# AdaLN block with channel attention and a mixture of experts: normalisations moved from VectorE to ScalarE, and the tail of attention computed through one extra weight product

## What is computed

```python
mod = (silu(c) @ wmod).reshape(16, 6, 1, 128)          # sa, ca, ga, sb, cb, gb per batch
h   = layernorm(x) * (1 + ca) + sa
q, k, v = h @ Wq.T + bq, h @ Wk.T + bk, h @ Wv.T + bv  # 16 heads of 8 channels
q = softmax over the 8 channels of a head;  k = softmax over the 512 tokens
state = k^T v per head (8 x 8);  o = q state           # 128 channels again
o = (o - mean(o)) * rsqrt(var(o) + eps) * ln_g + ln_b
x = x + ga * (o @ Wo.T + bo)
h = layernorm(x) * (1 + cb) + sb
x = x + gb * moe(h)                                    # 8 experts 128->128 (gelu)->128, top 2 of 8
```

## Time and profile before

| | us |
|---|---|
| median of 3 runs | 433.97 (433.52 to 435.66) |
| the profiled execution, its own time | 437.05 |
| its span | 435.1 |
| PE, DVE busy | 386.1 (89%), 347.0 (80%) |
| ACT, POOL busy | 250.5 (58%), 214.7 (49%) |
| distance of two steps in the loop | 48.6 |

### The profile page before, as it was taken

How to read it: one execution, slowest core, us unless ns; L and a number is a source line. 1 busy time by engine, 2 the same in 40 slices (tenths; PEclk the granted TensorE clock), 3 DMA queues, 4 the chain that set the end, 5 groups by cost and what they waited for, 6 DMA issues and landing times.

```text
span 435.1 us, 8603 instructions
## 1 busy us (share of the span) xinstructions
PE 386.1 (89%) x2660; PEld 343.7 (79%) x2660; DVE 347.0 (80%) x1176; ACT 250.5 (58%) x390; POOL 214.7 (49%) x222
## 2 busy tenths in 40 slices
PE   4545858998999999998989999998989999999995
PEld 3444656988988888888979888888889888989895
DVE  4577889888898989888888988898888889885631
ACT  2433447565657476575667485675667475675541
POOL 3421525364545465464645465464645564664442
PEclk9968589899999999999999999999999999999999
DMA  6720023060505124160605033140605042234160
GB/s 198 264 94 28 2 89 133 2 219 26 218 26 177 66 68 150 35 207 24 218 24 205 37 103 116 49 194 25 217 24 194 26 141 80 95 127 164 58 217 26
DMA packets 17787, 47.51 MB, mean 109 GB/s; under 512 B 2067, under 2 KB 4966, under 8 KB 17510
## 3 DMA queue, kind: packets, MB, share of 16 engines
q1 hardware_dynamic: 17568, 46.84, 30.5%
q10 hardware_dynamic: 198, 0.41, 0.2%
HBM read 42.76 MB, written 4.48 MB: 109 GB/s over the span
## 4 chain that ended last, share of the span: by engine, by line
PE 34%; DVE 30%; issue 15%; POOL 5%; ACT 5%; DVEq 1%; POOLq 0%; ACTq 0%
PE pY L626 14%; DVE xn L758 4%; PE pH L614 3%; DVE top L857 3%; PE pH L615 3%; PE pH L616 3%; DVE v L883 3%; ACT u L452 3%; DVE xn L846 2%; POOL rstd L347 2%; DVE qs L782 2%; DVE qmax L778 2%; DVE kmax L764 2%; POOL v L335 2%; DVE qs L773 2%
## 5 line engine op out<-in xcount | busy, mean ns | idle before, releaser
L626 PEld LDWEIGHTS pY<-wout,v 128*128 128x128 f32 x1024 | 127.4, 191 | 9.1 <-DVE v L883 3.6
L626 PE MATMUL pY<-wout,v 128*128 128x128 f32 x1024 | 132.7, 276 | 1.3 <-DVE v L883 0.5
L452 ACT ACTIVATE u<-pH,cols 128x512 f32<-128x512 f32 x128 | 86.6, 686 | 63.6 <-PE pH L616 63.0
L883 DVE TENSOR_TENSOR v<-u,gate_bc 128x512 f32<-128x512 f32 x80 | 59.4, 745 | 24.6 <-ACT u L452 10.7
L335 POOL TENSOR_TENSOR v<-u,gate_bc 128x512 f32<-128x512 f32 x48 | 62.4, 1301 | 31.2 <-ACT u L452 13.0
L614 PE MATMUL pH<-h_hi,win_hi 128*128 128x512 f32 x128 | 59.5, 465 | 9.2 <-ACT u L452 9.2
L615 PE MATMUL pH<-h_hi,win_lo 128*128 128x512 f32 x128 | 51.0, 398 | 0.0
L616 PE MATMUL pH<-h_lo,win_hi 128*128 128x512 f32 x128 | 50.6, 395 | 0.0
L846 DVE TENSOR_SCALAR xn<-x_all,mv,rstd 128x128 f32 (+1 forms) x64 | 35.7, 619 | 14.0 <-POOL rstd L347 14.0
L325 POOL TENSOR_TENSOR rstd_o<-ve_o,neg_half 128x4 f32<-128x4 f32 x16 | 16.3, 1017 | 52.6 <-DVE ve_o L816 52.6
L347 POOL TENSOR_TENSOR rstd<-ve,neg_half 128x4 f32<-128x4 f32 x16 | 22.3, 1396 | 38.8 <-DVE ve L840 38.7
(11 more groups left out here) (142 smaller groups left out, 868.4 us busy)
## 6 DMA issues: line engine op xcount, KB each, us to landing
gate_bc<-route_scratch SPq DMA_DIRECT2D x64, 512.0 KB, 5.3
x_all<-in_L_attn_x SPq DMA_DIRECT2D x16, 256.0 KB, 6.4
out<-x_all SPq DMA_DIRECT2D x16, 256.0 KB, 2.0
gates<-gate_scratch SPq DMA_DIRECT2D x1, 2048.0 KB, 7.0
gb_bc<-gb_scratch SPq DMA_DIRECT2D x1, 1024.0 KB, 4.3
win<-in_L_ffn_w_in SPq DMA_DIRECT2D x1, 512.0 KB
wout<-in_L_ffn_w_out SPq DMA_DIRECT2D x1, 512.0 KB
wmod_sb<-in_L_wmod ACTq DMA_DIRECT2D x1, 384.0 KB, 3.6
```

Of the source, the lines that this page charges most:

```text
L452: act.activation(u[:, e % U, :], pH[:, e % 2, :], ACT.Gelu_apprx_tanh, bias=cols[:, e:e + 1]).then_inc(s["gelu_done"], 1)
L626: i = mm(pY[:, t * P:(t + 1) * P], v[:, e % U, t * P:(t + 1) * P], wout[:, e, :], start=False, stop=(e == NE - 1), skip_group_check=True)
L883: dve.tensor_tensor(v[:, e % U, :], u[:, e % U, :], gate_bc[:, par, e, :], ALU.mult).then_inc(s["v_done"], 1)
```

## The change

Every line below is from the diff; a line of "..." stands where it is cut.

- The two applications of a normalisation leave DVE (`tensor_scalar`, subtract mean, multiply) and become four ACT activations each, Identity with a per-partition scale (rstd) and bias (minus mean times rstd). DVE computes that bias in one small operation (`ln1_offset`, `ln2_offset`). On ACT, `ln1_apply(b+4)` stands between gelu 4 and gelu 5, `ln2_apply(b+2)` at the end of the step, so ahead of gelu 0 of the next step.
- `state` gives the transposed state; DVE only masks it (`s2T`). A new PE product, `state_weights`, multiplies it by two matrices side by side, [centred, gained and gated output weight | centring matrix]; ACT scales the 256 columns by 1/sum and brings them to SBUF (`sw_evac`). `attend` then takes turned q as weights, one tile of tokens at a time, against each half: the centred output goes to pQT (first), the projection to pC, both token-major.
- ACT squares the centred output, DVE sums it (`tensor_reduce`); `ssq`, `project`, `outT_evac` and the steps L804 to L812 go.
- The value bias is added where v is brought to SBUF, by DVE (`v_bias`) in place of ACT (`v_evac`).
- `qv` of the next batch now waits for the square (its bank is used for the centred output).
- In the setup, the output weight gets its centring by one more product, for which PE and DVE wait.

```diff
 (pool, rstd_L and rstd_B)
+                w(pool, "xn1_ready", T * n)
...
+                w(pool, "xn2_ready", T * n)
 (pool, gated_const)
-                pool.tensor_tensor(wog[:, :], wo_gain[:, :], gates[:, n, 0, :], ALU.mult).then_inc(s["wog_ready"], 1)
+                w(pool, "sw_done", n)
+                pool.tensor_tensor(sw_rhs[:, 0, :], wo_gain[:, :], gates[:, n, 0, :], ALU.mult).then_inc(s["wog_ready"], 1)
 (act)
+            def ln1_apply(n):
+                act.wait_ge(s["nmr1_ready"], n + 1)
+                w(act, "hT_done", n)
+                for t in range(T):
+                    act.activation(xn1[:, t, :], x_all[:, n, t, :], ACT.Identity, bias=nmr1[:, t:t + 1], scale=rstd1[:, t:t + 1]).then_inc(s["xn1_ready"], 1)
...
-            def v_evac(n):
...
-                act.activation(sq[:, :], pC[:, :], ACT.Square).then_inc(s["sq_ready"], 1)
-                act.activation(outT[:, :], pC[:, :], ACT.Copy).then_inc(s["outT_ready"], 1)
+            def sw_evac(n):
+                act.wait_ge(s["sw_done"], n + 1)
+                act.wait_ge(s["kinv_ready"], n + 1)
+                w(act, "out_done", 2 * n)
+                act.activation(sw[:, :, :].rearrange("p a c -> p (a c)"), pSW, ACT.Copy, scale=kinv[:, 0:1]).then_inc(s["sw_ready"], 1)
+
+            def out_square(n):
+                act.wait_ge(s["out_done"], 2 * n + 1)
+                w(act, "ssum_done", n)
+                act.activation(sq[:, :, :].rearrange("p t c -> p (t c)"), pQT, ACT.Square).then_inc(s["sq_ready"], 1)
 (act, step)
                 if B:
                     h2_evac(b + 1, nxt)
+                if A2:
+                    sw_evac(b + 2)
                 if M:
                     gelu(b, 2)
                     gelu(b, 3)
                 if A2:
-                    outT_evac(b + 2)
+                    out_square(b + 2)
...
                 if M:
                     gelu(b, 4)
+                if L:
+                    ln1_apply(b + 4)
+                if M:
                     gelu(b, 5)
-                if A1:
-                    v_evac(b + 3)
...
                     qT_evac(b + 3)
+                if A2:
+                    ln2_apply(b + 2)
 (pe)
             def qv(n):
-                w(pe, "qT_ready", n)
+                w(pe, "sq_ready", n)
...
-                    i = mm(pS, ek[:, t, :], v_sb[:, t, :], start=(t == 0), stop=(t == T - 1))
+                    i = mm(pS, v_sb[:, t, :], ek[:, t, :], start=(t == 0), stop=(t == T - 1))
+            def state_weights(n):
+                pe.wait_ge(s["s2T_ready"], n + 1)
+                pe.wait_ge(s["wog_ready"], n + 1)
+                mm(pSW, s2T[:, :], sw_rhs[:, :, :].rearrange("p a c -> p (a c)"), start=True, stop=True).then_inc(s["sw_done"], 1)
             def attend(n):
-                pe.wait_ge(s["s_ready"], n + 1)
+                pe.wait_ge(s["sw_ready"], n + 1)
                 pe.wait_ge(s["qT_ready"], n + 1)
-                mm(pC[:, :], s3[:, :], qT[:, :], start=True, stop=True).then_inc(s["out_done"], 1)
+                for half, o in ((1, pQT), (0, pC)):
+                    for t in range(T):
+                        i = mm(o[:, t * P:(t + 1) * P], qT[:, t * P:(t + 1) * P], sw[:, half, :], start=True, stop=True)
+                    i.then_inc(s["out_done"], 1)
 (pe, step)
                     combine(b - 1, nxt, 5)
+                if A2:
+                    state_weights(b + 2)
                 if B:
                     h2T(b + 1)
...
-                if A2:
-                    ssq(b + 2)
...
-                if A2:
-                    project(b + 2)
 (dve)
-            def ln1_apply(n):
+            def ln1_offset(n):
                 dve.wait_ge(s["rstd1_ready"], n + 1)
+                w(dve, "xn1_ready", T * n)
+                dve.scalar_tensor_tensor(out=nmr1[:, :], in0=mv1[:, :, 0], scalar=-1.0, in1=rstd1[:, :],
+                                         op0=ALU.mult, op1=ALU.mult).then_inc(s["nmr1_ready"], 1)
...
+            def v_bias(n):
+                dve.wait_ge(s["qv_done"], n + 1)
+                w(dve, "state_done", n)
+                dve.tensor_tensor(v_sb[:, :, :], pQV[:, :, 1, :], bv_bc[:, :].unsqueeze(1).to_broadcast([P, T, P]),
+                                  ALU.add).then_inc(s["v_ready"], 1)
...
+                dve.tensor_tensor(s2T[:, :], pS, blockmask[:, :], ALU.mult).then_inc(s["s2T_ready"], 1)
...
-                dve.wait_ge(s["ssq_done"], n + 1)
-                dve.tensor_scalar(ve_o[:, :], pSSQ, 1.0 / C, LN_EPS, ALU.mult, ALU.add).then_inc(s["veo_done"], 1)
+                dve.wait_ge(s["sq_ready"], n + 1)
+                dve.tensor_reduce(ssum[:, :], sq[:, :, :], AX.X, ALU.add).then_inc(s["ssum_done"], 1)
+                dve.wait_ge(s["ssum_done"], n + 1)
+                dve.tensor_scalar(ve_o[:, :], ssum[:, :], 1.0 / C, LN_EPS, ALU.mult, ALU.add).then_inc(s["veo_done"], 1)
...
                     q_shift(b + 3)
+                    v_bias(b + 3)
                 if A2:
                     out_var(b + 2)
 (dve, setup; pe has the product between)
+                dve.tensor_scalar(gain[:, :], woT[:, :], cols[:, NE + 1:NE + 2], None, ALU.mult).then_inc(s["gain_ready"], 1)
+                dve.tensor_scalar(cen[:, :], ident[:, :], 1.0 / C, None, ALU.subtract).then_inc(s["cen_ready"], 1)
+                dve.tensor_scalar(sw_rhs[:, 1, :], ident[:, :], 1.0 / C, None, ALU.subtract)
+                dve.wait_ge(s["mm_gain"], 1)
+                dve.tensor_copy(wo_gain[:, :], pA[:, 0:P]).then_inc(s["wo_gain_ready"], 1)
```

More of the change, by code:

```diff
@@ L67, in adaln_block @@
         woT = sb("woT", [P, P])
+        gain = sb("gain", [P, P])
         wo_gain = sb("wo_gain", [P, P])
@@ L412, in h2_evac, with ln2_apply @@
                 act.activation(h2_hi[:, par, :], pB[:, :], ACT.Identity, bias=modB[:, par, 1:2], scale=modB[:, par, 0:1]).then_inc(s["h2hi_ready"], 1)
+            def ln1_apply(n):
[3 more added lines that the diff above has]
+                    act.activation(xn1[:, t, :], x_all[:, n, t, :], ACT.Identity, bias=nmr1[:, t:t + 1], scale=rstd1[:, t:t + 1]).then_inc(s["xn1_ready"], 1)
+            def ln2_apply(n):
+                act.wait_ge(s["nmr2_ready"], n + 1)
+                w(act, "h2T_done", n)
+                for t in range(T):
+                    act.activation(xn2[:, t, :], x_all[:, n, t, :], ACT.Identity, bias=nmr2[:, t:t + 1], scale=rstd2[:, t:t + 1]).then_inc(s["xn2_ready"], 1)
             def exp_k(n):
@@ L513, in _ @@
             pe.wait_ge(s["attn_w_ready"], 2)
+            pe.wait_ge(s["gain_ready"], 1)
+            pe.wait_ge(s["cen_ready"], 1)
+            mm(pA[:, 0:P], cen[:, :], gain[:, :], start=True, stop=True).then_inc(s["mm_gain"], 1)
+            pe.wait_ge(s["wo_gain_ready"], 1)
             def router_here():
@@ L603, in gate_turn @@
                 pe.wait_ge(s["gate2_ready"], n + 1)
-                w(pe, "veo_done", n + 2 if not isinstance(n, int) else min(n + 2, NB))
                 for t in range(T):
@@ L840, in ln2_var, with ln2_offset @@
                 dve.tensor_scalar(ve2[:, :], mv2[:, :, 1], LN_EPS, None, ALU.add).then_inc(s["ve2_done"], 1)
-            def ln2_apply(n):
+            def ln2_offset(n):
                 dve.wait_ge(s["rstd2_ready"], n + 1)
-                w(dve, "h2T_done", n)
-                for t in range(T):
-                    dve.tensor_scalar(xn2[:, t, :], x_all[:, n, t, :], mv2[:, t, 0:1], rstd2[:, t:t + 1],
-                                      ALU.subtract, ALU.mult).then_inc(s["xn2_ready"], 1)
+                w(dve, "xn2_ready", T * n)
+                dve.scalar_tensor_tensor(out=nmr2[:, :], in0=mv2[:, :, 0], scalar=-1.0, in1=rstd2[:, :],
+                                         op0=ALU.mult, op1=ALU.mult).then_inc(s["nmr2_ready"], 1)
             def route(n):
@@ L909, in step @@
                 if L:
-                    ln1_apply(b + 4)
+                    ln1_offset(b + 4)
                 if M:
@@ L943, in step @@
                 if A2:
-                    ln2_apply(b + 2)
+                    ln2_offset(b + 2)
             def moe_gates_here():
```

67 lines of the change are left out of this document (17 added, 50 removed).

## The result

The changed kernel takes 441.74 us in the median of four runs (440.5 to 444.11), against 433.88 for the kernel before in the same comparison (433.52 to 435.66, four runs): a ratio of 1.0165, interval 1.0117 to 1.0213. It is slower by 1.65%, and outside my range of 423 to 439. The profiled executions took 441.16 (after) and 437.05 (before); the latter stood 3.1 above its median, so between the two traces only 3.8 us of span can be explained, and the medians say 7.9.

A forecast was written before the change was run, and what follows sets the result against it. PE, 95% busy, nearly bounds the loop, alongside a chain of waits through DVE and ACT. Loop 12 x -0.52, end -0.4, start +2.4: -4.2 on 437.05 gives 432.8, or 430.3 against the median; own range 428 to 433, full range 423 to 439.

The forecast's parts named there:

- Stretch 2: PE from the start of `hidden` 6 to the end of the next `kT`: 12.77 us plus 0.43 for `state_weights`, 13.20.
- PE without a gap: Claim that PE works through the 12.77 us from `hidden` 6 to the end of the next `kT` without waiting.
- worth nothing by itself: Claim that taking `ln2_apply` and the masking and scaling chain off DVE gains nothing there, as PE was the chain.
- Stretch 1: From the end of `kT` to `hidden` 6, through DVE and ACT: 11.52 us less 0.95 for the first normalisation, 10.57.
- A: Rival: DVE reaches kshift before POOL starts `h2_low`, saving 1.0 of kshift; loop about 23.1, time 422 to 424; chance 0.15.
- So the PE saving stays unused: Between `kT` and `hidden` 6, PE's work falls to about 9.5 us, but the chain stays with DVE and ACT.
- Activations: The four ACT activations of one normalisation: 0.46 us each at 0.35 distance, 1.5 us together.
- fit by 0.3 to 0.4: Gelu 0 ends 19.7 us after `kT`, `h_lo` at 22.4, before `hidden` 2 (20.0) and the next `kT` (22.8) need them.
- rival B: The loop's gain is eaten by late logits or gelu 0: period 24.0 to 24.2, time 434; chance 0.20.
- Rival C: ACT becomes the loop, `ln2_apply` delaying gelu 0 and `kT`: period near 24.5, time 440, slower; chance 0.20.
- Start: Steps before the full loop: +1.75 in step -2, +3.1 in step -1, -2.5 in step 0, together +2.4 us.
- End: After the loop, PE's work, one more step with A2: -0.4 us.

The follow-up runs named there:

- e1: The changed kernel run again with nothing altered: 444.02 us, ratio 1.0206 to the kernel before.
- e2: The changed kernel with POOL making the gained weight of the next batch before the second rstd: 436.84 us, ratio 1.0034 to the kernel before.
- e3: The kernel before with only the two normalisations moved to ACT, old tail of attention kept: 426.5 us, ratio 0.9797.
- e5: The kernel before with only the first normalisation moved to ACT: 427.48 us, ratio 0.9815.
- e10: The kernel of e3 with kbmax and kshift made one operation with a single SBUF input: 422.26 us, ratio 0.971 to the kernel before.
- e11: The kernel of e8 with kbmax and kshift made one operation with a single SBUF input: 424.06 us, ratio 0.9734 to the kernel before.
- e6: The kernel before with only the second normalisation moved to ACT: 436.64 us, ratio 1.0038.
- e8: The kernel of e2 with DVE's value bias moved behind the router's gates: 435.32 us, ratio 0.9988 to the kernel before.

## Why the prediction was wrong

By its steps, in the profiled executions:

- *Stretch 2, "12.77 + 0.43 = 13.20": this is the step that failed.* It counted the 0.43 us of `state_weights` and no wait in front of it. Of its two inputs I looked at neither: I did not ask when POOL's product L321 is ready once its reader moves to the head of the stretch, though POOL's order was before me. Before, that product ended at 211.78 and `state_weights` would have stood at 212.86; by the forecast's own shifts (the second rstd 0.1 later after `kT`, PE 0.95 earlier) that leaves 0.05 to spare, so even my own numbers would have shown a place with nothing in reserve. Measured are waits of 0.76 and 0.25 in turn, on average 0.50 (0.67 counted by starts), and a stretch 2 of 13.86 and 13.35, on average 13.60. In the medians the wait is worth 7.2 us beside e1, and 5.7 by the ratios to before (1.0165 and 1.0034, of 434), of the 11.4 by which 430.3 was missed; in the eleven steps of the traces it is 2.9 of the 6.4 that they miss (11 x 0.58).
- *That 13.20 is near the 13.26 of e2 is luck.* Two errors cancel in it. The base of 12.77 was not "PE without a gap": it held 0.31 of waiting for DVE, which goes with the second normalisation (12.46 in e3), where the prediction has it "worth nothing by itself". And behind `state_weights`, which takes 0.43 as forecast when it need not wait, stand 0.18 for gelu 0 and 0.18 for `h_lo`: 12.46 + 0.43 + 0.36 = 13.25.
- *Stretch 1, "11.52 - 0.95 = 10.57": right in kind, short by 0.2.* The exponential of q comes 203.02 - 194.94 = 8.08 after `kT`, for 7.89. I took kshift as unchanged, and in the step shown it was; but kbmax ahead of it, 0.20 before, became 0.36, and in the other kind of step 1.10 with a kshift of 0.16. A freed DVE reaches POOL's last operations one operation sooner, and then waits for their ends. e5 shows the same with nothing else changed. Taking the pair out is worth 0.55 a step in e10 and 1.0 in e11, with the order of `weigh` 2 and `h2_low` in it. I had put A, the rival in which the lock falls away, down to luck with the order; kshift's hold has to be removed by hand, and what is then left is a matter of the order, in e10 of 0.02 to 0.05 us.
- *"So the PE saving stays unused": right.* `hidden` 6 waits 1.48 for gelu 4, for the "about 1" of the forecast (0.78 before).
- *Activations, "1.5" for four: 1.63 to 1.65.* Single ones took 477 to 503 ns, and `sw_evac` 0.48. The Trainium skill's estimate (ScalarE: Activation LUTs, What ACT_TABLE_LOAD costs), which the prediction gave beside my own, was the better one; the trace agrees with it to a hundredth. The activations of `ln2_apply` and what follows, in the timelines of ACT, POOL and PE of the changed kernel:

```profile
213.04 1.65 ACT L428 ACTIVATE xn<-x_all,nmr,rstd 128x128 f32 x4 [1.49 <-DVE nmr L862]
214.60 0.67 ACT L470 ACTIVATE u<-pH,cols 128x512 f32<-128x512 f32 x1
...
216.67 1.28 POOL L346 TENSOR_TENSOR h_lo<-h,h_hi 128x512 fp32r<-128x512 f32 x1 [1.54 <-ACT h_hi L409]
...
218.62 0.48 PE L558 MATMUL pA<-h_hi,wk_hi 128*128 128x512 f32 x1
```

- *Gelu 0 and `h_lo` "fit by 0.3 to 0.4": wrong by about 0.5, and hidden by the wait.* Gelu 0 ends at 215.27, 20.3 after `kT` (forecast 19.7), and `h_lo` at 217.95, 23.0 after it (forecast 22.4). In the changed kernel `kT` still starts at 218.62 without a wait, but only because PE itself was held up at `state_weights`. In e2, where it was not, both come too late, by 0.18 each. That is the mechanism of rival B, on top of the one that no rival had. Rival C, in which ACT becomes the loop and whose time of 440 comes near the measured one, did not happen. C had the sign right and the mechanism wrong: moving the normalisations to ACT is the half that pays (e3). The Trainium skill's rule against it (ScalarE: Activation LUTs, Rules for kernel authors) does not hold for this kernel: with both on ACT e3 ran at 0.9797 of before, while ACT went from 58% busy to 69%. For the second move alone it is not contradicted: e6 took 436.64, no gain.
- *Start "+2.4": 2.3, with some luck.* Its parts were +1.75, +3.1 and -2.5, at the starts of `k_max` +0.85, +3.7 and -2.3. In e1, the same kernel, the sum was +4.1 (99.54 - 95.44), so the hit to a tenth is not more than one execution. In step -1 the row that I wrote down in advance is what the timeline of ACT shows, one behind the other:

```profile
67.39 1.65 ACT L428 ACTIVATE xn<-x_all,nmr,rstd 128x128 f32<-128x128 f32 x4 [0.91 <-DVE nmr L862]
69.06 1.28 ACT L470 ACT_TABLE_LOAD   x1
```

- *End "-0.4": +1.5, a miss of 1.9.* At the end of the profile `state_weights` waits for POOL too (the longest of the waits row, 1.4). In e8, with the weight made early and the value bias moved, what follows the last `k_max` takes 71.7, the 71.8 of before.
- *The sum against one execution.* The forecast of 432.8 was for an execution that began at 437.05 and was measured as 441.16. The further 3.1 us that I took off, to come to the median, did not apply to the changed kernel: its profiled execution stood 0.6 below its own median.

By the traces, then, the forecast for the execution missed by 8.4: 6.2 of gain in the loop that did not come, 1.9 at the end, 0.3 outside the span, and nothing at the start.

In short: half of the change gains 8.5 us, the other costs 15 to 18, some two fifths of it one wait of PE for a product of POOL that used to be needed late. Without that wait the eleven steps still take 8.3 us more than in e3 (264.89 for 256.62), and stretch 2 accounts for it: 13.26 for 12.46, `state_weights` itself and two short waits. In the medians the new tail costs 8.8 in e8 over e3, and 1.8 in e11 over e10, because without the pair of small operations its shorter work on PE in stretch 1 comes into use.

## What to carry to other kernels

When a change gives an operand a new reader, or moves its reader forward, follow each input of the new reader back through its producer's queue, even where that producer is at 49% and its operation is unchanged: slack belongs to a pair of writer and reader, not to an engine. And when a wait is removed, look for the next ones behind it: here half of its length came back. A change of two halves is worth timing in halves; here the sum hid a gain of 2% under a loss of about 4%. And where a small operation is many times longer than its size explains and ends with another engine's, time gained ahead of it is lost in it, until its form (number of inputs) or the other engine's order is changed; the hold may then pass to the next operation that can be held, as in e10.
